# A macaron layer on one core: the passes reordered, attention dealt to them in whole blocks of 128 tokens

## The chip, the cores and the metric

The kernel runs on 1 core of a Trainium2 chip. The metric is the device time of one execution in microseconds, the median of several runs. Everything is float32; products are made of float32 values split in a high and a low half.

## What is computed

The reference, cut to what matters (B 4, S 1024, D 512, 16 heads of 32, hidden size 2048):

```
def attn(x):                      # per token: 16 heads attend to each other
    q, k, v = (x @ wq.T), (x @ wk.T), (x @ wv.T)      # each (b, s, 16, 32)
    q, k = apply_rope(q), apply_rope(k)
    scores = einsum('bshd,bstd->bsht', q, k) / sqrt(32)
    return einsum('bsht,bstd->bshd', softmax(scores), v).reshape(b, s, 512) @ wo.T

def ffn(x):                       # fwht: normalized Walsh-Hadamard transform
    hidden = fwht(silu(x @ W1.T) * (x @ W3.T))
    return hidden @ W2.T

x = x + 0.5 * ffn(layernorm(x))
x = x + attn(layernorm(x))
x = x + 0.5 * ffn(layernorm(x))
```

The scores of a token are 16 x 16, over its own heads. So attention has no matrix product to speak of beside its projections, and its scores and mixtures are made on VectorE.

## The kernel before

**Tiles, blocks, passes.** The 4096 tokens are 8 tiles of 512; a tile has 4 blocks of 128 tokens. Each tile goes through a feed-forward twice, so there are 16 passes over the feed-forward weights, numbered 0 to 15. Pass 0 also prepares the weights (the transform is folded in the down weights, all are split in two halves and stored to memory). The order is tile 0's first feed-forward, then by turns the first one of tile i (pass 2i-1) and the second one of tile i-1 (pass 2i), and at last the second one of tile 7 (pass 15).

**A pass.** It has 16 steps, one for each 128 of the 2048 hidden values. TensorE does the up step (24 matmuls of 128x512 into PSUM `gu`: W1 and W3, 4 parts of the depth, 3 products of halves), and then the down step of the step before (12 matmuls into `acc`). Between them ScalarE makes silu (L573, `gated`), VectorE the product with the linear half (L807), ScalarE the high half (L579, `hid`) and VectorE the low half (L811). The down step waits for the low half. The up step n waits for the product of step n-2, whose PSUM it takes. The weights come from memory in each step over the queue of SP.

**Between two passes** ("the gap") stand, for the tiles that are due, the transposes of the normalised rows (L386), the output projection of a tile's attention (`wo`), the projections of queries, keys and values (`qkv`), and on VectorE the sums, the norms (L831, L836, L840; GpSimd makes the inverse root, L737 and L739), the low halves (L817) and the rotation of queries and keys (`rope`, L1005 to L1010).

**Attention of a block** is 16 pieces on VectorE: 8 of scores (a product of 128x1024, L257, and a sum over 32, L862), then the softmax (L870, L871, the exponential on ScalarE L614, L877, L878), then 8 of mixtures (L260 and L864), and a division (L882). The pieces stand between the feed-forward's instructions. `ffn` of the loop's passes has two blocks (`attention_sub`, 8 steps each). Passes 1 and 14 have all four blocks of a tile (`attention_dense`): there GpSimd makes 12 of each block's 16 products (`SHARED`, `shared_products`) and VectorE sums them.

**What sets the order.** Each engine's program is written out by hand and waits on counting semaphores; passes 2 to 13 stand in a loop over tiles (`Fori(2, LAST)`), whose body is `iteration`.

Of the kernel before, what the change touches and what calls it, by code (L numbers as in the profile page):

```python
# [7 lines left out]
FP32 = mybir.dt.float32  # L8
# [6 lines left out]
HEADS = 16  # L15
# [17 lines left out]

class Count:


    def __init__(self, sem):
        self.sem, self.start, self.k = sem, 0, 0

    def mark(self, ins):  # L40
        ins.then_inc(self.sem, 1)
        self.k += 1
        return self.start + self.k
# [9 lines left out]
def build(nc, x, up_raw, w2t, attn_raw, inv_freq, hadamard, identity, out):  # L53
    ctx = ExitStack()
    with ctx:
# [14 lines left out]

        down_stage = w_attn[:].rearrange("p m a k n -> p (m a k n)").rearrange("p (a n) -> p a n", a=HT)

        xt = [sb(f"xt{i}", [P, 2, KT, TOK], FP32R) for i in range(2)]
        hid = sb("hid", [P, 2, 2, TOK], FP32R)
        gated = sb("gated", [P, 2, TOK])
        x_in = sb("x_in", [P, SUBS, D])
        x_mid = sb("x_mid", [P, SUBS, D])
        x_out = sb("x_out", [P, SUBS, D])
# [10 lines left out]
        stats = sb("stats", [P, SUBS, 6])  # L89
        mean_var = sb("mean_var", [P, SUBS, 2])  # L90
        rstd = sb("rstd", [P, SUBS])
        eps = sb("eps", [P, SUBS])
        mixed = sb("mixed", [P, HEADS, HD])
        carrier = sb("carrier", [P, 64])
        minus_half = sb("minus_half", [P, SUBS])
# [6 lines left out]
        s_hada = sem("s_hada")  # L102
        s_w2 = [sem(f"s_w2_{c}") for c in range(len(W2_CUTS))]
        s_x = sem("s_x")
        s_first_x = [sem(f"s_first_x{s}") for s in range(SUBS)]
        s_attn_raw = [sem(f"s_attn_raw{m}") for m in range(4)]
# [5 lines left out]
        s_freq_out = sem("s_freq_out")  # L112

        s_tabs = sem("s_tabs")
# [23 lines left out]
        s_var_0 = sem("s_var_0")  # L138
        s_eps_0 = sem("s_eps_0")
        s_rstd_0 = sem("s_rstd_0")  # L140
        s_ln = sem("s_ln")
        s_ln_sub = sem("s_ln_sub")
        s_xt_ps = sem("s_xt_ps")
        s_xt_hi = sem("s_xt_hi")
        s_xt_lo = sem("s_xt_lo")
# [3 lines left out]
        s_mid = sem("s_mid")  # L149
# [7 lines left out]
        s_shared = sem("s_shared")  # L157
        s_summed = sem("s_summed")
# [6 lines left out]

        LAST = TILES - 1
# [4 lines left out]
        HADAMARD_FROM = 7  # L173

        def raw_hidden(n):

            at = RAW.index(n)
            if at < SUBS:
                return x_out[:, at, :]
            if at < 2 * SUBS:  # L180
                return x_mid[:, at - SUBS, :]
            return prod[:, 2, (at - 2 * SUBS) * TOK:(at - 2 * SUBS + 1) * TOK]
# [17 lines left out]
        def turns_at_once(l):  # L200

            return l + 1 if isinstance(l, int) and l == 0 else l

# [3 lines left out]

        EVEN = ((3, 3, 2), (1, 3, 2, 2, 0))  # L210
        PIECES = HEADS // 2
# [6 lines left out]
        def dense_order():  # L218

            order = []  # L220
            for s in range(SUBS):
                order += [(s, u) for u in range(AHEAD if s else 0, PIECES)]
                if s + 1 < SUBS:
                    order += [(s + 1, u) for u in range(AHEAD)]
                order += [(s, PIECES + u) for u in range(PIECES)]

            at = order.index((SUBS - 1, PIECES))
            held = order.index((SUBS - 1, AHEAD)) - AHEAD
            return order[:held] + order[held + AHEAD:at] + order[held:held + AHEAD] + order[at:]

# [3 lines left out]
        def tok_at(slot):  # L234

            if isinstance(slot, int):
                return heads(tok[:, slot, :])
            return tok[:, bass.ds(slot, 1), :].rearrange("p o (h d) -> p (o h) d", h=HEADS)

        def values_at(slot):  # L240

            if isinstance(slot, int):
                return tok[:, slot, :].rearrange("p (d t) -> p d t", d=HD)
            return tok[:, bass.ds(slot, 1), :].rearrange("p o (d t) -> p (o d) t", d=HD)

        def product_buffer(b):

            if b < 3:
                return prod[:, b, :]
            return tok[:, 12 + 2 * (b - 3):14 + 2 * (b - 3), :].rearrange("p a n -> p (a n)")  # L250

        def unit_products(eng, s, u, buf, half=0):

            g = 2 * (u % PIECES)
            if u < PIECES:
                q, k = tok_at(2 * s), tok_at(2 * s + 1)
                return eng.tensor_tensor(product_buffer(buf).rearrange("p (h t d) -> p h t d", h=2, t=HEADS),  # L257
                                         wide(q[:, g:g + 2, None, :], 2, HEADS), wide(k[:, None, :, :], 1, 2), ALU.mult)
            v = values_at(8 + s)
            return eng.tensor_tensor(product_buffer(buf).rearrange("p (h d t) -> p h d t", h=2, d=HD),  # L260
                                     wide(scores[:, half, g:g + 2, None, :], 2, HD), wide(v[:, None, :, :], 1, 2), ALU.mult)
# [6 lines left out]
        def _(sp):  # L268
# [9 lines left out]
            for s in range(SUBS):  # L278
                sp.dma_start(x_in[:, s, :], x_v[0][:, s, :]).then_inc(s_first_x[s], 16)
# [6 lines left out]
            sp.dma_start(freq[:], wide(inv_freq.rearrange("(a f) -> a f", a=1), 0, P)).then_inc(s_freq_out, 16)  # L286
# [9 lines left out]
            for j in range(HT):  # L296
                keep_up(j, j % 2, j + 2 < HT)

# [45 lines left out]
            with sp.Fori(1, 2 * TILES) as b:  # L344
                weights(b)
# [3 lines left out]
        def _(pe):  # L349
# [6 lines left out]
            def xt_ready(build, k, needed=True):  # L356

                if needed:
                    pe.wait_ge(s_xt_lo, 4 * build + k + 1)

            def up(n, u, X, build=None):
                for w in range(2):
                    for k in range(KT):
                        xt_ready(build, k, build is not None and w == 0)
# [17 lines left out]
            def transposes(src, bank, ks):  # L382

                for k in ks:
                    for s in range(SUBS):
                        ins = nc.tensor.transpose(bank[:, k, s * P:(s + 1) * P], tok[:, src(s), k * P:(k + 1) * P], ident[:])  # L386
                    ins.then_inc(s_xt_ps, 1)

            def transposes_by_sub(src, bank, sub_ready):

                for s in range(SUBS):
                    sub_ready(s)
                    for k in range(KT):
                        ins = nc.tensor.transpose(bank[:, k, s * P:(s + 1) * P], src(s, k), ident[:])
                        if s == SUBS - 1:
                            ins.then_inc(s_xt_ps, 1)

            def sub_normed(l):

                return lambda s: pe.wait_ge(s_ln, l + 1) if s == SUBS - 1 else pe.wait_ge(s_ln_sub, (SUBS - 1) * l + s + 1)  # L400

            def normed(s, k):
                return tok[:, 12 + s, k * P:(k + 1) * P]

            def ffn(b, X, x_build, before_build=None, src=None, dense=None, values=None):

                n0 = HT * b

                def up_step(jj, u, x_build=None):
                    pe.wait_ge(s_up_loaded[u], 16 * (HT // 2 * (b - 1) + jj + 1))
                    up(n0 + 2 * jj + u, u, X, x_build)

                def down_step(jj, u, first, last):
                    pe.wait_ge(s_down_loaded[u], 16 * (HT // 2 * (b - 1) + jj + 1))
                    down(n0 + 2 * jj + u, u, first, last)

                if values is not None:
                    pe.wait_ge(s_v, values - 2)  # L420
                up_step(0, 0, x_build)
                if values is not None:
                    pe.wait_ge(s_v, values)
                up_step(0, 1)
                pe.wait_ge(s_added, SUBS * b)
                down_step(0, 0, True, False)
                with pe.Fori(1, HT // 2) as jj:
                    for u in range(2):
                        pe.wait_ge(s_h, n0 + 2 * jj + u - 1)
                        up_step(jj, u)  # L430
                        down_step(jj - 1 + u, 1 - u, False, False)
                if dense is not None:
                    down_step(HT // 2 - 1, 1, False, True)
                    pe.wait_ge(s_h, n0 + HT)
# [813 lines left out]
```

## Time and profile before

| | |
|---|---|
| median of 3 runs | 2620.24 us (2619.89 to 2620.66) |
| profiled execution, own time | 2618.36 us |
| its span, first to last instruction | 2616.6 us |
| mean granted TensorE clock | 0.99 |
| TensorE matmuls busy | 97% of the span |
| VectorE busy | 76% |
| ScalarE busy | 21% |
| GpSimd busy | 12% |

Matmuls are pipelined, so that a busy share of TensorE says only that it was not idle. The distance from one matmul's start to the next says how long one takes.

### The profile page before, as it was taken

What the parts mean: (1) busy time and instruction counts of PE and PEld (TensorE: products, weight loads), DVE (VectorE), ACT (ScalarE), POOL (GpSimd) and SP (SyncE); (2) the same over time, 40 slices, a digit from 0 to 9 for tenths busy, and PEclk for the clock granted to TensorE, in tenths of its full rate; (3) what the DMA queues carried; (4) which work ended last, traced back from release to release, by engine and by line L of the source; (5) the groups of instructions that cost most, each with busy time, mean ns of one, the idle gap of its engine ahead of it and who ended that gap; (6) DMA issues with size and microseconds to landing.
All of it is one profiled execution on the core that took longest, in us unless ns stands there. A gap on an engine that the chain in (4) does not pass through costs nothing.

```text
span 2616.6 us, 32355 instructions
## 1 busy us (share of the span) xinstructions
PE 2544.9 (97%) x11328; PEld 2099.1 (80%) x11328; DVE 1991.0 (76%) x2494; ACT 539.6 (21%) x829; POOL 320.9 (12%) x164
## 2 busy tenths in 40 slices
PE   8989989999999999999999999999999999998799
PEld 6867768888888888888888888888888888877687
DVE  7668997777887777778777778877778777879712
ACT  3312221122111211222112211112121121122111
POOL 0046850000000000000000000000000000168400
PEclk9999999999999999999999999999999999999899
DMA  9643423555335551455515554255533555144254
GB/s 307 233 177 123 167 96 113 192 205 193 115 142 194 198 195 74 181 193 199 192 64 193 204 192 168 88 193 208 192 136 120 192 209 192 73 150 155 97 192 168
DMA packets 91644, 437.05 MB, mean 167 GB/s; under 512 B 8896, under 2 KB 15296, under 8 KB 58304
## 3 DMA queue, kind: packets, MB, share of 16 engines
q1 hardware_dynamic: 83616, 420.65, 43.9%
q10 hardware_dynamic: 7968, 15.73, 1.7%
q8 instruction: 21, 0.34, 0.1%
q14 instruction: 39, 0.32, 0.0%
HBM read 402.79 MB, written 33.55 MB: 167 GB/s over the span
## 4 chain that ended last, share of the span: by engine, by line
PE 83%; DVE 14%; issue 1%; SPq 1%; POOL 1%; DMA 0%; ACT 0%; POOLq 0%; DVEq 0%; ACTq 0%
PE gu L352 19%; PE gu L354 19%; PE gu L353 19%; PE acc L352 8%; PE acc L354 8%; PE acc L353 8%; DVE mixed L864 3%; DVE prod L260 2%; DVE scores L862 2%; DVE hid L811 1%; PE gu L386 1%; DVE prod L257 1%; DVE gated L807 1%; DVE xt L817 1%; PE acc L463 1%
## 5 line engine op out<-in xcount | busy, mean ns | idle before, releaser
L352 PE MATMUL gu<-xt,w_up 128*128 128x512 f32 x2048 | 800.6, 391 | 3.6 <-DVE xt L817 3.6
L353 PE MATMUL gu<-xt,w_up 128*128 128x512 f32 x2048 | 798.2, 390 | 0.0
L354 PE MATMUL gu<-xt,w_up 128*128 128x512 f32 x2048 | 797.9, 390 | 0.0
L352 PEld LDWEIGHTS gu<-xt,w_up 128*128 128x128 f32 x2048 | 385.4, 188 | 85.8 <-DVE xt L817 3.0
L807 DVE TENSOR_TENSOR gated<-gated,gu 128x512 f32<-128x512 f32 x240 | 164.0, 683 | 375.6 <-ACT gated L573 375.6
L354 PEld LDWEIGHTS gu<-xt,w_up 128*128 128x128 f32 x2048 | 385.2, 188 | 80.3
L353 PEld LDWEIGHTS gu<-xt,w_up 128*128 128x128 f32 x2048 | 385.4, 188 | 80.0
L352 PE MATMUL acc<-w_down,hid 128*128 128x512 f32 x960 | 383.7, 400 | 35.6 <-DVE hid L811 35.6
L573 ACT ACTIVATE gated<-gu 128x512 f32<-128x512 f32 x240 | 143.5, 598 | 1149.5 <-PE gu L354 1149.4
L353 PE MATMUL acc<-w_down,hid 128*128 128x512 f32 x960 | 380.0, 396 | 0.0
L354 PE MATMUL acc<-w_down,hid 128*128 128x512 f32 x960 | 379.9, 396 | 0.0
L260 DVE TENSOR_TENSOR prod<-scores,tok 128x1024 f32<-128x1024 f32 x216 | 295.3, 1367 | 0.8
L864 DVE TENSOR_REDUCE mixed<-prod 128x64 f32<-128x1024 f32 x224 | 265.6, 1212 | 1.7
L862 DVE TENSOR_REDUCE scores<-prod 128x32 f32<-128x1024 f32 x224 | 264.7, 1210 | 0.5
L257 DVE TENSOR_TENSOR prod<-tok 128x1024 f32 (+1 forms) x200 | 252.4, 1262 | 6.9 <-DVE scores L862 0.8
L352 PEld LDWEIGHTS acc<-w_down,hid 128*128 128x128 f32 x960 | 183.8, 191 | 81.2 <-DVE hid L811 35.2
L737 POOL TENSOR_TENSOR rstd<-mean_var,eps 128x4 f32<-128x4 f32 x23 | 4.6, 199 | 1925.2 <-DVE mean_var L836 1925.2
L579 ACT ACTIVATE hid<-gated 128x512 fp32r<-128x512 f32 x240 | 152.0, 633 | 423.9 <-DVE gated L807 421.8
L354 PEld LDWEIGHTS acc<-w_down,hid 128*128 128x128 f32 x960 | 184.1, 192 | 39.2
L353 PEld LDWEIGHTS acc<-w_down,hid 128*128 128x128 f32 x960 | 184.2, 192 | 37.6
L811 DVE TENSOR_TENSOR hid<-gated,hid 128x512 fp32r<-128x512 f32 x240 | 177.2, 738 | 44.7 <-ACT hid L579 44.7
L352 PE MATMUL gu<-w_attn,xt 128*128 128x512 f32 x512 | 201.3, 393 | 8.0 <-DVE xt L817 3.8
(122 smaller groups left out, 2188.3 us busy)
## 6 DMA issues: line engine op xcount, KB each, us to landing
w_up<-up_pairs SPq DMA_DIRECT2D x240, 1024.0 KB, 4.8
w_down<-down_pairs SPq DMA_DIRECT2D x240, 512.0 KB, 3.4
up_pairs<-w_up SPq DMA_DIRECT2D x16, 1024.0 KB, 4.8
prod<-up_raw SPq DMA_DIRECT2D x16, 512.0 KB, 5.8
down_pairs<-w_attn SPq DMA_DIRECT2D x4, 2048.0 KB, 17.7
x_in<-x ACTq DMA_DIRECT2D x7, 1024.0 KB, 5.3
out<-x_out ACTq DMA_DIRECT2D x7, 1024.0 KB, 4.6
tok<-attn_raw SPq DMA_DIRECT2D x4, 1024.0 KB, 18.8
```

What stands on the lines that cost most here:

```text
L257: return eng.tensor_tensor(product_buffer(buf).rearrange("p (h t d) -> p h t d", h=2, t=HEADS), wide(q[:, g:g + 2, None, :], 2, HEADS), wi ...
L260: return eng.tensor_tensor(product_buffer(buf).rearrange("p (h d t) -> p h d t", h=2, d=HD), wide(scores[:, half, g:g + 2, None, :], 2, HD ...
L352: nc.tensor.matmul(o, w_hi, m_hi, start=first, stop=False)
L353: nc.tensor.matmul(o, w_hi, m_lo, start=False, stop=False)
L354: return nc.tensor.matmul(o, w_lo, m_hi, start=False, stop=last)
L386: ins = nc.tensor.transpose(bank[:, k, s * P:(s + 1) * P], tok[:, src(s), k * P:(k + 1) * P], ident[:])
L573: nc.scalar.activation(gated[:, u, :], gu[:, 2 * u, :], ACT.Silu).then_inc(s_silu, 1)
L579: nc.scalar.activation(hidden(u)[0], gated[:, u, :], ACT.Copy).then_inc(s_hid_hi, 1)
L807: nc.vector.tensor_tensor(gated[:, u, :], gated[:, u, :], gu[:, 2 * u + 1, :], ALU.mult).then_inc(s_h, 1)
L811: nc.vector.tensor_tensor(low, gated[:, u, :], high.bitcast(FP32), ALU.subtract)\
L862: return nc.vector.tensor_reduce(scores[:, half, g:g + 2, :], product_buffer(buf).rearrange("p (h t d) -> p h t d", h=2, t=HEADS), AX.X, A ...
L864: return nc.vector.tensor_reduce(mixed[:, g:g + 2, :], product_buffer(buf).rearrange("p (h d t) -> p h d t", h=2, d=HD), AX.X, ALU.add)
```

## The change

**The passes** follow a table `PASSES` (1 or 2 for the feed-forward, and the tile): 1.0, 1.1, 1.2, 2.0, 1.3, 2.1, 1.4, 2.2, 1.5, 2.3, 1.6, 1.7, 2.4, 2.5, 2.6, 2.7. So pass 2 is now a first feed-forward and pass 3 the second one of tile 0. `WO_AT` says in which gap a tile's output projection stands. Where the pass behind that gap is the second feed-forward of the same tile (`LATE`, passes 3, 5, 7, 14, 15), its norm is made in the gap (`late_gap`); for all other passes the norm of the next tile is made beside the steps of the pass before, in steps 8, 9, 11 and 12 (`beside`), and its transposes stand before the last down step (`early_gap`).

**Attention** is dealt by `LAST_SUB` (the last block whose projections are made before pass p) and `UNITS_TO` (pieces done by the end of pass p). Each of the passes 1 to 14 has 32 pieces, two whole blocks, but passes 2, 5, 8 and 12, which have 48, three blocks. `AHEAD` is 0: no block is begun before the one ahead of it is done. All pieces are made on VectorE; the code for GpSimd's products is gone. A planner (`units_by_step`) spreads a pass's pieces over its steps 0 to 14. A block that is projected first in its gap has its norm made in the pass before where its tile allows it (`early_subs`, one or two blocks, steps 10 and 13).

**The rest.** Four tiles of residuals stay on the chip (`xs`) in place of `x_in`, `x_mid` and `x_out`, so ScalarE's copy of a tile (L660) is gone and a tile is loaded some passes ahead. All programs but the inner steps of TensorE and SP are written out with constant waits, without a loop. At the start TensorE runs 24 matmuls on zeros (`WARM`), and the second tile is loaded in the middle of pass 0.

```diff
+PASSES = ((1, 0), (1, 1), (1, 2), (2, 0), (1, 3), (2, 1), (1, 4), (2, 2),
+          (1, 5), (2, 3), (1, 6), (1, 7), (2, 4), (2, 5), (2, 6), (2, 7))
+WO_AT = {3: 0, 5: 1, 7: 2, 8: 3, 10: 4, 12: 5, 14: 6, 15: 7}
+LATE = tuple(p for p, t in WO_AT.items() if PASSES[p] == (2, t))
+LAST_SUB = (None, 2, 4, 6, 8, 11, 13, 15, 18, 20, 22, 24, 27, 29, 31)
+UNITS_TO = (0, 32, 80, 112, 144, 192, 224, 256, 304, 336, 368, 400, 448, 480, 512)
+AHEAD = 0
+def units_by_step(p):
+    mine, steps = list(UNITS.get(p, ())), []
+    beside = [0.0] * HT
+    if p + 1 < NP and p + 1 not in LATE:
+        for n, cost in ((X_STATS, 1.4), (X_STATS + 1, 2.0), (X_APPLY, 1.1), (X_APPLY + 1, 1.1)):
+            beside[n] += cost
+    beside[Q_STATS] += 0.85 * len(early_subs(p + 1))
+    beside[Q_APPLY] += 0.55 * len(early_subs(p + 1))
+    unit = 2.5
+    total, spent = sum(beside) + unit * len(mine), 0.0
+    for n in range(HT):
+        spent += beside[n]
+        now = []
+        while mine and n < STEPS and (n == STEPS - 1 or spent + unit / 2 <= total * (n + 1) / STEPS):
+            now.append(mine.pop(0))
+            spent += unit
+        steps.append(tuple(now))
...
-        SHARED = 3 * ((0, 1, 3, 4, 5, 6, 7, 9, 10, 12, 14, 15),) + ((0, 1, 3, 4, 5, 6, 7, 9, 10, 12, 13, 15),)
-        POOL_BUFFERS = 3
-        AHEAD = 4
...
+            pe.wait_ge(s_zeros, 1)
+            for _ in range(WARM):
+                nc.tensor.matmul(acc[:, 0, :], hid[:, 0, 0, 0:P], hid[:, 0, 0, :], start=True, stop=True)
...
+            def attention(p):
+                mine = UNITS.get(p, ())
+                free, made = [chain.k] * 2, {}
...
+                for at, (g, u) in enumerate(mine):
+                    if u == PIECES:
+                        row_sums(g)
+                    if at not in made:
+                        make(at)
+                    if at + 1 < len(mine) and mine[at + 1][1] not in (0, PIECES):
+                        make(at + 1)
+                    dve.wait_ge(s_dve, made.pop(at))
+                    free[at % 2] = chain.mark(unit_sum(g, u, at % 2))
+                    if u == PIECES - 1:
+                        shift(g, free[at % 2])
+                    if u == 2 * PIECES - 1:
+                        divide(g, free[at % 2])
+                    yield
...
+                for n in range(HT):
+                    u, count = n % 2, len(STEP_UNITS[p][n])
+                    dve.wait_ge(s_silu, n0 + n + 1)
+                    nc.vector.tensor_tensor(gated[:, u, :], gated[:, u, :], gu[:, 2 * u + 1, :], ALU.mult).then_inc(s_h, 1)
+                    unit(min(count, 1))
...
+                    dve.wait_ge(s_hid_hi, n0 + n + 1)
+                    high, low = hidden(u)
+                    nc.vector.tensor_tensor(low, gated[:, u, :], high.bitcast(FP32), ALU.subtract).then_inc(s_hid_lo, 1)
+                    unit(count - min(count, 1))
+                    beside(n)
```

`make` is a product into one of two buffers, `unit_sum` its sum. VectorE in pass 1, one step and the start of the next. Before, in a packed pass, with products that GpSimd has made (a sum that reads `tok` or `prod` without a product ahead of it):

```order
L807 TENSOR_TENSOR gated<-gated,gu 128x512
L862 TENSOR_REDUCE scores<-tok 128x32
L811 TENSOR_TENSOR hid<-gated,hid 128x512
L862 TENSOR_REDUCE scores<-tok 128x32
L257 TENSOR_TENSOR prod<-tok 128x1024
L862 TENSOR_REDUCE scores<-prod 128x32 x2
L807 TENSOR_TENSOR gated<-gated,gu 128x512
```

The change, same pass:

```order
L1381 TENSOR_TENSOR gated<-gated,gu 128x512
L1136 TENSOR_TENSOR prod<-tok 128x1024 x2
L1148 TENSOR_REDUCE scores<-prod 128x32
L1388 TENSOR_TENSOR hid<-gated,hid 128x512
L1136 TENSOR_TENSOR prod<-tok 128x1024
L1148 TENSOR_REDUCE scores<-prod 128x32
L1381 TENSOR_TENSOR gated<-gated,gu 128x512
```

Four sums and one product a step became two sums and their own products.

VectorE in pass 2 of the change, a step with four pieces of a block, between two products of the hidden values (L1381):

```order
L1381 TENSOR_TENSOR gated<-gated,gu 128x512
L1136 TENSOR_TENSOR prod<-tok 128x1024
L1148 TENSOR_REDUCE scores<-prod 128x32
L1388 TENSOR_TENSOR hid<-gated,hid 128x512
L1136 TENSOR_TENSOR prod<-tok 128x1024
L1148 TENSOR_REDUCE scores<-prod 128x32
L1136 TENSOR_TENSOR prod<-tok 128x1024
L1148 TENSOR_REDUCE scores<-prod 128x32
L1136 TENSOR_TENSOR prod<-tok 128x1024
L1148 TENSOR_REDUCE scores<-prod 128x32
L1381 TENSOR_TENSOR gated<-gated,gu 128x512
```

Before, the fullest steps of pass 2 have three pieces; now steps of three and four take turns through the whole pass, one piece between the product and the low half (L1388) and the others behind it.

## Rows read from the trace of the kernel before

**Rows 1.** The page: busy time, and the granted clock in 40 slices.

```profile
PE 2544.9 (97%) x11328; PEld 2099.1 (80%) x11328; DVE 1991.0 (76%) x2494; ACT 539.6 (21%) x829; POOL 320.9 (12%) x164
...
PEclk9999999999999999999999999999999999999899
```

**Rows 2.** Timeline of TensorE, down, up, down; last from the chain, a tile's transposes.

```profile
540.92 0.39 PE L352 MATMUL acc<-w_down,hid 128*128 128x512 f32 x1
...
543.64 0.39 PE L352 MATMUL gu<-xt,w_up 128*128 128x512 f32 x1
...
549.08 0.39 PE L352 MATMUL acc<-w_down,hid 128*128 128x512 f32 x1
...
712.73 1.75 PE acc L386 x16
```

**Rows 3.** Windows: passes 1, 14, one loop turn, a plain pass; clock, DMA last.

```profile
213.87:372.73 158.86, 141.66 (x576) 113.32 (x577) 153.05 (x135) 31.88 (x46) 131.60 (x48) 0.94 0.44 159
2298.34:2458.00 159.66, 141.52 (x578) 113.54 (x577) 152.29 (x133) 32.00 (x45) 124.64 (x45) 0.94 0.44 158
400.60:712.73 312.13, 312.03 (x1410) 259.13 (x1409) 243.12 (x312) 63.84 (x97) 3.62 (x6) 1.00 0.46 168
...
552.00:684.00 132.00, 132.00 (x592) 109.58 (x591) 102.69 (x114) 27.76 (x42) 0.00 (x0) 1.00 0.54 198
```

**Rows 4.** Waits, whole run, TensorE: total, times, longest.

```profile
PE acc L352 <- DVE hid L811: 35.6, 15, 5.1
```

**Rows 5.** Timeline of TensorE behind passes 1 and 14, the idle time in brackets.

```profile
376.32 0.50 PE L352 MATMUL gu<-w_attn,xt 128*128 128x512 f32 x1 [1.68 <-DVE xt L817]
...
2461.59 0.50 PE L352 MATMUL gu<-w_attn,xt 128*128 128x512 f32 x1 [1.68 <-DVE xt L817]
```

**Rows 6.** Timeline of VectorE in a plain pass: a step, then a softmax.

```profile
570.87 0.68 DVE L807 TENSOR_TENSOR gated<-gated,gu 128x512 f32<-128x512 f32 x1
571.47 1.22 DVE L257 TENSOR_TENSOR prod<-tok 128x1024 f32 x1
...
579.09 0.68 DVE L807 TENSOR_TENSOR gated<-gated,gu 128x512 f32<-128x512 f32 x1
...
584.93 0.42 DVE L870 TENSOR_REDUCE head_max<-scores 128x16 f32<-128x256 f32 x1
...
585.72 0.68 DVE L807 TENSOR_TENSOR gated<-gated,gu 128x512 f32<-128x512 f32 x1
...
588.83 0.42 DVE L877 TENSOR_REDUCE head_sum<-scores 128x16 f32<-128x256 f32 x1 [1.03 <-ACT scores L614]
...
589.51 1.23 DVE L260 TENSOR_TENSOR prod<-scores,tok 128x1024 f32<-128x1024 f32 x1
```

**Rows 7.** Groups by line and form, whole run: busy us, mean ns, idle before.

```profile
L257 DVE TENSOR_TENSOR prod<-tok 128x1024 f32 x192 | 234.1, 1219 | 6.9 <-DVE scores L862 0.8
...
L573 ACT ACTIVATE gated<-gu 128x512 f32<-128x512 f32 x240 | 143.5, 598 | 1149.5 <-PE gu L354 1149.4
...
L257 DVE TENSOR_TENSOR prod<-tok 128x1024 f32<-128x1024 f32 x8 | 18.3, 2292 | 0.0
...
L882 DVE TENSOR_TENSOR tok<-mixed,head_sum 128x512 f32 x24 | 16.6, 692 | 0.8
```

**Rows 8.** Timeline of VectorE in a gap: a tile's statistics and its normalisation.

```profile
417.07 2.46 DVE L831 BATCH_NORM_STATS2 stats<-x_in 128x6 f32<-128x512 f32 x4
...
421.47 1.92 DVE L840 TENSOR_SCALAR tok<-x_in,mean_var,rstd 128x512 f32<-128x512 f32 x4 [1.40 <-POOL rstd L739]
```

**Rows 9.** Timeline of TensorE in the last gap.

```profile
2477.49 3.65 PE L394 MATMUL acc<-ident,tok 128*128 128x128 f32 x16 [4.68 <-DVE tok L840]
```

**Rows 10.** Pass 0: TensorE's first and third up steps; a low half, from the chain.

```profile
15.71 0.80 PE L352 MATMUL gu<-xt,w_up 128*128 128x512 f32 x1 [2.56 <-DVE xt L817]
...
29.15 0.40 PE L352 MATMUL gu<-xt,w_up 128*128 128x512 f32 x1
...
27.66 1.22 DVE w_up L1015
```

More of the change, by code:

```diff
@@ new lines @@
+UNITS = units_by_pass()
+X_STATS, X_APPLY, Q_STATS, Q_APPLY = 8, 11, 10, 13
+STEPS = HT - 1
+def units_by_step(p):
[15 more added lines that the diff above has]
+        steps.append(tuple(now))
+    assert not mine
+    return tuple(steps)
@@ new lines, with exps @@
+STEP_UNITS = {p: units_by_step(p) for p in range(1, NP)}
+def exps():
+    place = {}
+    for p in range(1, NP):
+        for n, units in enumerate(STEP_UNITS[p]):
+            for g, u in units:
+                place[g, u] = p, n
+    behind, ahead = {}, {}
+    for g in range(TILES * SUBS):
+        made, used = place[g, PIECES - 1], place[g, PIECES]
+        if made == used:
+            behind.setdefault(made, []).append(g)
+        else:
+            ahead.setdefault((made[0], made[1] + 1), []).append(g)
+    return behind, ahead
@@ new lines, with transposed @@
+EXP_BEHIND, EXP_AHEAD = exps()
+X_ORDER = (2, 3, 0, 1)
+def transposed():
+    order = [("x", 0, k) for k in range(KT)]
+    order += [("q", g, 0) for g in new_subs(1)] + [("x", 1, k) for k in range(KT)]
+    for p in range(2, NP):
+        new = new_subs(p)
+        att = [("a", WO_AT[p], k) for k in range(KT)] if p in WO_AT else []
+        if p in LATE:
+            order += att + [("q", g, 0) for g in new[:2]] + [("x", p, k) for k in range(KT)]
+        else:
+            order += [("q", g, 0) for g in early_subs(p)] + [("x", p, k) for k in X_ORDER]
+            order += [("q", g, 0) for j, g in enumerate(new[:2]) if not is_early(p, j)] + att
+        order += [("q", g, 0) for g in new[2:]]
+    return {key: at for at, key in enumerate(order)}
@@ new lines, with normed_groups, group_subs @@
+TP = transposed()
+def normed_groups():
+    order = [("x", 0)] + [("q", g) for g in new_subs(1)] + [("x", 1)]
+    for p in range(2, NP):
+        if p not in LATE:
+            order.append(("x", p))
+        if early_subs(p):
+            order.append(("e", p))
+        late = [("x", p)] if p in LATE else []
+        order += late + [("q", g) for j, g in enumerate(new_subs(p)) if not is_early(p, j)]
+    return order
+def group_subs(key):
+    if key[0] == "x":
+        return tuple(range(SUBS))
+    return early_subs(key[1]) if key[0] == "e" else (key[1],)
@@ new lines, with ln_of_sub, sub_slots @@
+GROUPS = normed_groups()
+GROUP = {key: at for at, key in enumerate(GROUPS)}
+LN_FROM = dict(zip(GROUPS, itertools.accumulate([len(group_subs(key)) for key in GROUPS], initial=0)))
+def ln_of_sub(g):
+    p = next(p for p in range(1, len(LAST_SUB)) if g in new_subs(p))
+    j = new_subs(p).index(g)
+    return LN_FROM["e", p] + early_subs(p).index(g) + 1 if is_early(p, j) else LN_FROM["q", g] + 1
+def sub_slots():
+    free, held, slots = {a: None for a in range(12)}, {}, {}
+    for p in range(1, len(LAST_SUB)):
+        for g in list(held):
+            if len(held[g]) == 3 and all((g, 2 * PIECES - 1) != unit for q in range(p, len(LAST_SUB)) for unit in UNITS[q]):
+                for a in held[g][1:]:
+                    free[a] = ("s", g)
+                held[g] = held[g][:1]
+        if p in WO_AT:
+            for g in range(SUBS * WO_AT[p], SUBS * WO_AT[p] + SUBS):
+                free[held.pop(g)[0]] = ("a", WO_AT[p])
+        for g in new_subs(p):
+            mine = [a for a in free][:3]
+            slots[g] = tuple((a, free.pop(a)) for a in mine)
+            held[g] = tuple(mine)
+    return slots
@@ new lines, in x_of, with ln_column, ln_columns, normed @@
+        def x_of(g):
+            return residual(g // SUBS)[:, g % SUBS, :]
+        def ln_column(key):
+            if key[0] == "x":
+                return 0
+            if key[0] == "q" and key[1] in new_subs(1):
+                return 4 + key[1]
+            return 4 if key[0] == "e" else 6
+        def ln_columns(key):
+            return set(range(ln_column(key), ln_column(key) + len(group_subs(key))))
+        def normed(s):
+            return tok[:, 12 + s, :]
+        def sub_normed(g):
+            p = next(p for p in range(1, len(LAST_SUB)) if g in new_subs(p))
+            j = new_subs(p).index(g)
+            if p == 1:
+                return normed(j)
+            return prod[:, 2, (j % 2) * D:(j % 2 + 1) * D]
@@ L398, in sub_normed @@
[L398 to L434, printed above, removed]
-                    transposes_by_sub(lambda s, k: tok[:, 2 * s, k * P:(k + 1) * P], gu,
-                                      lambda s: pe.wait_ge(s_attn, dense + s + 1))
-                    return
-                if before_build is not None:
-                    before_build()
-                    pe.wait_ge(s_h, n0 + HT - 1)
-                    transposes(src, gu, (0, 1))
-                    pe.wait_ge(s_h, n0 + HT)
-                    transposes(src, gu, (2, 3))
-                down_step(HT // 2 - 1, 1, False, True)
@@ new lines, in sub_high, with values @@
+            def sub_high(g):
+                split_high(sub_split(g)[0], sub_bank(g).rearrange("p (k t) -> p k t", k=KT), "q", g, 0)
+            def values(g):
+                slot, before = SLOTS[g][2]
+                if before is not None and before[0] == "a":
+                    act.wait_ge(s_tp, TP["a", before[1], KT - 1] + 1)
+                if before is not None and before[0] == "s":
+                    act.wait_ge(s_attn, before[1] + 1)
+                act.wait_ge(s_v_ps, g + 1)
+                nc.scalar.activation(tok[:, slot, :], v_bank(g), ACT.Copy).then_inc(s_v, 1)
@@ new lines, in gap @@
+            def gap(p):
+                new = new_subs(p)
+                if p in LATE:
+                    attention_high(p)
+                    for g in new[:2]:
+                        sub_high(g)
+                    for k in range(KT):
+                        x_high(p, k)
+                else:
+                    for k in X_ORDER:
+                        x_high(p, k)
+                    for j, g in enumerate(new[:2]):
+                        if not is_early(p, j):
+                            sub_high(g)
+                    if p in WO_AT:
+                        attention_high(p)
+                for j, g in enumerate(new):
+                    values(g)
+                    if j == 0 and len(new) > 2:
+                        sub_high(new[2])
@@ new lines, in sub_low, with ln_stats, ln_means @@
+            def sub_low(g):
+                high, low = sub_split(g)
+                split_low(low, sub_bank(g).rearrange("p (k t) -> p k t", k=KT), high, "q", g, 0)
+            def ln_stats(key, s, src):
+                at = ln_column(key) + s
+                return chain.mark(nc.vector.bn_stats(stats[:, at, :], src))
+            def ln_means(key, mark, same_columns):
+                dve.wait_ge(s_dve, mark)
+                if same_columns is not None:
+                    dve.wait_ge(s_ln, LN_FROM[same_columns] + len(group_subs(same_columns)))
+                for s in range(len(group_subs(key))):
+                    at = ln_column(key) + s
+                    ins = nc.vector.bn_aggr(mean_var[:, at, :], stats[:, at, :])
+                ins.then_inc(s_var, 1)
@@ L1212, in hadamard_128, with j_of @@
+            def j_of(p, g):
+                return new_subs(p).index(g)
+            feed_forward(1)
+            for p in range(2, NP):
+                if p in LATE:
+                    late_gap(p)
+                else:
+                    early_gap(p)
+                feed_forward(p)
+            for s in range(SUBS):
+                add_sum(NP - 1, s)
 def hadamard_128():
```

1121 lines of the change are left out of this document (589 added, 532 removed).

## The prediction

> **What bounds the kernel now.** I read the page first: TensorE is busy 97% of the span, VectorE 76%, GpSimd 12%, and the granted clock is 9 or more in every slice but one [rows 1]. So almost all of the time is matmuls, and what a change can move is the rest. Next the timeline of TensorE in a plain pass: the first matmul of a down step starts at 540.92, the first of the following up step at 543.64, the next down step at 549.08 [rows 2]. Twelve matmuls take 2.72 us, 36 take 8.16, so one is 0.2267 us and a pass of 16 steps 130.6. Then the stretches. The 16 transposes of a tile take 1.75 us [rows 2]. One turn of the loop (two passes, 1344 matmuls and 64 transposes) is 312.13 us with TensorE busy for 312.03 of it, at clock 1.00 [rows 3]: the plain passes have nothing to lose. Passes 1 and 14 are different. They hold four blocks of attention each, take 158.86 and 159.66 us for the work of 130.6, at a mean clock of 0.94, and VectorE is busy for 153.05 and 152.29 of it [rows 3]. VectorE is the bound there, and the list of waits says so: TensorE waits for the low half of the hidden values 15 times, 35.6 us, up to 5.1 each [rows 4]. After each of these passes TensorE waits another 1.68 us [rows 5]. That is all the attention costs today: 28.3 + 29.1 + 3.4 = 60.8 us.
>
> In a plain pass VectorE is busy for 102.69 us of 132 [rows 3]: two blocks leave some 29 us free. This is the number that the change turns on.
>
> **The change, part by part.**
>
> *Passes 1 and 14 hold two blocks.* They become plain passes, 130.6 us each. I take off the whole 60.8. This needs that a two-block pass without the old code is still hidden. Its VectorE work for steps 0 to 14: 32 pieces, each a product and a sum. A step from 570.87 to 579.09 holds the product and low half of the hidden values and three pieces [rows 6]; behind a product of 128x512 the next instruction starts 0.6 us later, so a piece is (8.22 - 1.2) / 3 = 2.34 us. 32 pieces are 75 us, 15 steps' own two instructions 18, the two softmaxes 6, norms 7: 106 against 15 x 8.16 = 122.4. Hidden on average. Within a step: from the end of an up step to the low half go silu 0.6 [rows 7], product 0.68, one piece 2.34 and a low half like the product, 4.3 us, while TensorE has 5.44 us of the next up step to do. 1.1 us are in hand. I cost it at nothing; the rival "short passes wait" prices it otherwise.
>
> *Passes 2, 5, 8 and 12 hold three blocks, on VectorE alone.* For pass 5, whose successor's rows and two early blocks are also normalised in it:
> - 48 pieces x 2.34 = 112.3 us;
> - per block the maximum and subtraction from 584.93 to 585.72, 0.79, the row sum and reciprocal from 588.83 to 589.51, 0.68 [rows 6], the division 0.69 [rows 7]: 3 x 2.16 = 6.5;
> - the wait for the exponential, 1.03 us in the plain pass [rows 6]. Two of three blocks have theirs issued in the same step, so 2; the third stands behind the next silu, which is early when VectorE is late;
> - the step's own two instructions, 15 x 1.2 = 18;
> - the next tile's statistics 2.46 and its normalisation 1.92 [rows 8], with 0.4 for the means 4.8; two early blocks, half of that, 2.4.
>
> The sum is 146.0 us for steps 0 to 14. To the start of the last down step comes silu before (0.7) and the last product, copy and low half behind (2.1): 148.8. TensorE alone needs for the same stretch 122.4 us and the transposes of a tile and two blocks, 1.75 + 2 x 0.44: 125.1 (rounded up). Excess 23.7 us. Pass 12 is alike. Pass 8 has one early block, 1.2 less work and 0.4 less transposes: 22.9. Pass 2 has no next tile to normalise (the one after it is late), 4.8 and 0.9 less: 19.8. Sum of the four: 90.1 us. Nothing is carried over into the gap between passes: the pieces of a pass end in its step 14, and VectorE's work in the gap (a block's rope is the like of six instructions of 0.6 us, 3.6) lies beside 36 matmuls, 8.2 us, of projections a block.
>
> What could make that smaller: if all 29.3 us that VectorE has free in a plain pass could be used, the third block's 16 x 2.34 + 2.16 + 1.0 = 40.6 would push TensorE by 11.3 us alone, 45 for the four. But a part of that free time lies at the pass's first up step and in its last, where no piece stands. What could make it larger: passes 1 and 14 ran at a mean clock of 0.94 [rows 3], which is some 12% of 159 us at 1.2 instead of 2.4 GHz, 9.6 us of matmul time each. If it all lay on the path in each long pass, 4 x 9.6 = 38 us on top. The long pass leaves TensorE idle as these do, but VectorE sets the pace, so only the last down steps count: I take 0.5 each, 2 us.
>
> *GpSimd makes no products.* In passes 1 and 14 VectorE's own products took 2.29 us, in the plain ones 1.22 [rows 7]. After the change nearly all should take 1.22. The Trainium skill (SBUF — State Buffer, "Who interferes with whom") says that a VectorE instruction with two SBUF inputs contends with a GpSimd instruction that reads SBUF, which would make the two means one cause. By another cause, a crowded pass as such, the 48 products of a long pass would cost 1.07 us more each, 51 us a pass, and the sum would be some 200 us higher; the plain passes, with GpSimd idle and 1.22, speak against it.
>
> *A figure against my step.* The Trainium skill (TensorE: Matmul & The Clock Gate, "Wait — 56ns, not 53.3ns?") has warm matmuls of 512 columns start 215.7 ns apart. By it a pass would be 124.2 us, not 130.6, and each long pass would exceed TensorE by 6.4 us more, 26 in all. The rows say 226.7 and I keep them.
>
> *The gaps.* Projections are the same number of matmuls in all, only spread otherwise. In a late gap the norm's chain must fit under one query and key projection of 5.44 us. From the last output projection: sum, statistics, means, GpSimd, normalisation: in the last gap of today this leaves TensorE 4.68 us idle before its transposes [rows 9], with nothing to cover it; in the new order 5.44 us cover it. Zero, but with under 1 us to spare. In pass 5's gap the third block's projection waits for a rope that stands behind the norm of that third block on VectorE. Counted in instructions of 0.6 us, the second block's rope ends some 32.6 us into the gap, while TensorE has 30.3 us of matmuls before that projection: 2.3 us. The last gap (pass 15) has no cover in either order: zero change. The gap after pass 0 has one block less: zero beside the moved matmuls, within 3 us either way.
>
> *The start.* 24 matmuls on zeros run ahead of the first transposes. Today the first up step starts at 15.71 and the third at 29.15, while the third slab's low half, which that one needs, is made from 27.66 to 28.88 [rows 10]. So an earlier or faster start is worth 0.3 us at most. The second tile's load in the middle of pass 0 and the 1 us of setup: zero, up to 3 us dearer.
>
> *The unrolled code.* VectorE's and ScalarE's loops are written out. Their waits do not show any loop cost today (0.1 us idle in 312), so there is none to win.
>
> **The sum.** The profiled execution took 2618.4 us: 2618.4 - 60.8 + 90.1 + 2 + 2.3 = 2652.0. The median of the runs is 1.9 us above it. The short passes and the start may win or lose a microsecond. I say 2652.
>
> **The rivals.** 0.2% (5.2 us) is about what a measurement of this kernel can tell from no change.
> - *Forecast: the long passes are bound by VectorE at about 20 to 24 us each.* 2652; 2630 to 2675 with the small costs either way. Chance 0.62.
> - *The third block goes into VectorE's idle time.* The place is the same four passes, the price 11.3 us each: 2618.4 - 60.8 + 45 + 4.3 + 1.9 = 2609, faster. For it speaks that 29.3 us are free; against it that the order puts all pieces in steps 0 to 14, and that a step of 3.2 pieces and its share of the norms comes to 9.7 us against 8.16. It decides as soon as a long pass costs under 12.8 us (51 in all), which needs pieces of 2.1 us or less. Chance 0.10.
> - *The two sides cancel.* A long pass costs 12.8 to 15.4 us, which takes pieces of 2.15 us. 2620. Chance 0.08.
> - *Short passes wait as well.* Ten passes; in two steps of each a softmax stands between pieces. If the 1.1 us in hand is used up and each of these is 1 us late: 20 us more, 2672. TensorE's plain passes with 0.1 us idle and the same softmaxes speak against it. Chance 0.10.
> - *The clock falls in the long passes and it counts.* Up to 38 us more, 2690. Against it: TensorE waits there for VectorE, and half speed is hidden by the wait. Chance 0.10.
>
> Slower is the first and the last two, 0.82; same 0.08; faster 0.10. The range runs from 2622 to 2686.
>
> **What the changed profile would show.** Passes 1 and 14 at 130.6 us and without a wait of TensorE for the low half; four stretches of 147 to 151 us, in passes 2, 5, 8 and 12, in which VectorE is busy over 95% and TensorE waits some 1.5 us in every step; clock below 1.00 in them alone. VectorE's products all at 1.22. GpSimd without its 131.60 and 124.64 us in passes 1 and 14 [rows 3]. Wrong would be: long passes under 140 us (pieces cheaper than 2.34, or work in the gap), or waits in short passes, or a clock below 0.97 over the whole.

## The result

The changed kernel takes 2639.66 us, the median of 4 runs (2639.04 to 2641.03). The kernel before took 2620.06 beside it. The ratio is 1.0076, with a 95% interval of 1.0058 to 1.0093: slower by 19.6 us. The forecast was 2652, slower, with a range of 2622 to 2686. The profiled execution took 2639.04 us against 2618.36 before, 20.7 more; its span is 2637.3.

The page of the changed kernel: busy times, the clock, and the groups that answer to [rows 7].

```profile
PE 2552.0 (97%) x11352; PEld 2095.9 (79%) x11352; DVE 2018.9 (77%) x2570; ACT 523.8 (20%) x821; POOL 62.7 (2%) x90
...
PEclk9999999999999999999999999999999999999999
...
L551 PE MATMUL acc<-w_down,hid 128*128 128x512 f32 x960 | 384.0, 400 | 52.0 <-DVE hid L1388 51.0
...
L1136 DVE TENSOR_TENSOR prod<-tok 128x1024 f32<-128x1024 f32 x256 | 309.5, 1220 | 1.5
```

The shares of busy time [rows 1] hardly tell the two kernels apart: TensorE 97% and 97%. The wait of TensorE for the low half of the hidden values tells more: 51.0 us here, 35.6 before [rows 4].

Windows of the changed kernel, each from the first matmul of a pass to the start of its last down step: passes 2, 5, 8 and 12, then 3 and 1. Behind the length stand the busy time and the number of instructions of TensorE, of its weight loads, of VectorE, ScalarE and GpSimd, then the granted clock, the DMA share and GB/s.

```profile
353.22:499.05 145.83, 134.26 (x582) 108.03 (x580) 137.93 (x150) 30.12 (x45) 0.90 (x2) 0.99 0.48 173
857.51:1008.35 150.84, 136.10 (x590) 108.57 (x588) 145.03 (x168) 31.43 (x47) 2.11 (x4) 0.99 0.47 165
1361.30:1510.83 149.53, 134.54 (x585) 108.34 (x584) 142.88 (x161) 30.06 (x45) 1.95 (x4) 0.99 0.52 183
2017.58:2168.41 150.83, 136.93 (x590) 109.93 (x588) 144.28 (x165) 30.82 (x46) 2.10 (x4) 0.98 0.47 167
531.84:662.55 130.71, 130.65 (x589) 108.28 (x588) 105.58 (x127) 28.06 (x44) 2.10 (x4) 1.00 0.52 189
201.53:331.85 130.32, 130.26 (x586) 107.84 (x584) 104.06 (x123) 27.71 (x43) 1.95 (x4) 1.00 0.52 190
```

The two kinds stand apart at once. In the last two windows, with two blocks, TensorE is busy for all but 0.06 us and VectorE for 80 or 81% of the stretch. In the first four, with three blocks, VectorE is busy for 95 or 96% (137.93 of 145.83, 145.03 of 150.84), TensorE idle for 12 to 15 us, and the stretch 15 to 20 us longer than with two. Pass 1 needs 130.32 us where the packed pass before took 158.86 [rows 3]; that window holds the last down step (2.72 us) and no transposes, this one 20 transposes (2.2 us) and no last down step, so the two are comparable within a microsecond.

How VectorE's time goes in a long pass is seen in its timeline, pass 5 of the changed kernel: its first product, a step of four pieces, the step behind it with a block's softmax, and the product of the last step.

```profile
863.78 0.69 DVE L1381 TENSOR_TENSOR gated<-gated,gu 128x512 f32<-128x512 f32 x1 [4.74 <-ACT gated L917]
...
873.04 0.68 DVE L1381 TENSOR_TENSOR gated<-gated,gu 128x512 f32<-128x512 f32 x1
...
883.54 0.68 DVE L1381 TENSOR_TENSOR gated<-gated,gu 128x512 f32<-128x512 f32 x1
...
885.84 0.42 DVE L1157 TENSOR_TENSOR scores<-scores,head_max 128x256 f32<-128x256 f32 x1
886.18 0.69 DVE L1388 TENSOR_TENSOR hid<-gated,hid 128x512 fp32r<-128x512 f32 x1
886.78 0.41 DVE L1164 TENSOR_REDUCE head_sum<-scores 128x16 f32<-128x256 f32 x1
...
1005.72 0.68 DVE L1381 TENSOR_TENSOR gated<-gated,gu 128x512 f32<-128x512 f32 x1
```

The step takes 10.50 us where TensorE needs 8.16 [rows 2]. Less the 1.2 of the step's own two instructions, four pieces are 9.30, 2.33 each. Such a step is rarer than "steps of three and four take turns" says: the planner gives pass 5 three steps of four pieces and twelve of three; pass 2 has four steps of four. Between the first and the last of these rows VectorE waits for nothing. The row sum (L1164) starts without idle time in front of it: the exponential is done while the low half (L1388) is made.

### The profile page after: what moved, and what is told of

Read it like the earlier page. It is cut to its first block, busy times and chain, and to the rows that moved or that the text cites. A ratio compares the mean times of both kernels' runs of the same rounds, so it can differ in the third digit from the quotient of the medians.

```text
span 2637.3 us, 30195 instructions
## 1 busy us (share of the span) xinstructions
PE 2552.0 (97%) x11352; PEld 2095.9 (79%) x11352; DVE 2018.9 (77%) x2570; ACT 523.8 (20%) x821; POOL 62.7 (2%) x90
## 4 chain that ended last, share of the span: by engine, by line
PE 76%; DVE 21%; issue 1%; SPq 1%; ACT 0%; DMA 0%; POOLq 0%; DVEq 0%; POOL 0%; ACTq 0%
PE gu L551 16%; PE gu L553 16%; PE gu L552 16%; PE acc L551 8%; PE acc L553 8%; PE acc L552 8%; DVE scores L1148 4%; DVE prod L1141 4%; DVE mixed L1150 4%; DVE prod L1136 4%; DVE hid L1388 1%; DVE gated L1381 1%; PE gu L584 1%; PE acc L584 1%; PE acc L639 1%
## 5 line engine op out<-in xcount | busy, mean ns | idle before, releaser
L1381 DVE TENSOR_TENSOR gated<-gated,gu 128x512 f32<-128x512 f32 x240 | 163.9, 683 | 370.2 <-ACT gated L917 369.5
L1136 DVE TENSOR_TENSOR prod<-tok 128x1024 f32<-128x1024 f32 x256 | 309.5, 1220 | 1.5
L1148 DVE TENSOR_REDUCE scores<-prod 128x32 f32<-128x1024 f32 x256 | 310.0, 1212 | 0.0
L1150 DVE TENSOR_REDUCE mixed<-prod 128x64 f32<-128x1024 f32 x256 | 309.8, 1212 | 0.0
L1141 DVE TENSOR_TENSOR prod<-scores,tok 128x1024 f32<-128x1024 f32 x256 | 307.7, 1212 | 1.2
L551 PEld LDWEIGHTS acc<-w_down,hid 128*128 128x128 f32 x960 | 181.7, 189 | 109.2 <-DVE hid L1388 54.9
L553 PEld LDWEIGHTS acc<-w_down,hid 128*128 128x128 f32 x960 | 182.1, 190 | 38.8
L552 PEld LDWEIGHTS acc<-w_down,hid 128*128 128x128 f32 x960 | 182.1, 190 | 35.5
L1388 DVE TENSOR_TENSOR hid<-gated,hid 128x512 fp32r<-128x512 f32 x240 | 163.9, 683 | 15.0 <-ACT hid L925 14.7
L551 PE MATMUL gu<-w_attn,sub_xt 128*128 128x512 f32 x232 | 92.2, 397 | 7.2 <-DVE sub_xt L1020 4.5
L552 PE MATMUL gu<-w_attn,sub_xt 128*128 128x512 f32 x232 | 91.0, 392 | 0.0
```

The source lines that it names most:

```text
L551: nc.tensor.matmul(o, w_hi, m_hi, start=first, stop=False)
L552: nc.tensor.matmul(o, w_hi, m_lo, start=False, stop=False)
L553: return nc.tensor.matmul(o, w_lo, m_hi, start=False, stop=last)
L1136: return nc.vector.tensor_tensor(prod[:, buf, :].rearrange("p (h t d) -> p h t d", h=2, t=HEADS), wide(q[:, h:h + 2, None, :], 2, HEADS), ...
L1141: return nc.vector.tensor_tensor(prod[:, buf, :].rearrange("p (h d t) -> p h d t", h=2, d=HD), wide(scores[:, g % 2, h:h + 2, None, :], 2, ...
L1148: return nc.vector.tensor_reduce(scores[:, g % 2, h:h + 2, :], prod[:, buf, :].rearrange("p (h t d) -> p h t d", h=2, t=HEADS), AX.X, ALU.add)
```

## The experiments

**1. The same work, dealt evenly.** The projections, norms and passes stay; only the pieces move, so that blocks are begun in one pass and ended in the next.

```diff
-UNITS_TO = (0, 32, 80, 112, 144, 192, 224, 256, 304, 336, 368, 400, 448, 480, 512)
+UNITS_TO = (0, 37, 73, 110, 144, 183, 219, 256, 293, 329, 366, 400, 438, 475, 512)
```

> The changed kernel with the same 512 pieces dealt evenly, 34 to 39 in each of the passes 1 to 14, blocks begun in one pass and ended in the next; projections, norms and passes stay where they are. Theory A (all of the loss is the four passes that VectorE bounds, 76.6 us in the profile): 2640 - 77, and up to 6 us given back where a pass has 38 or 39 pieces: 2563 to 2570. Rival B (the loss comes with the new order, its gaps and late norms, and VectorE's total work): no pass is relieved in sum, 2630 or more. Rival C (a block split over two passes costs waits of its own for the exponential and the values): 2580 to 2600.

Measured: 2566.74 us, ratio to before 0.9796 (0.9779 to 0.9812). Windows of the same passes 2, 5, 8 and 12, to the start of the last down step:

```profile
355.62:485.44 129.82, 129.76 (x581) 107.43 (x580) 110.47 (x125) 30.30 (x45) 0.90 (x2) 1.00 0.51 190
844.10:974.81 130.71, 130.65 (x589) 108.24 (x588) 122.40 (x145) 28.07 (x44) 2.10 (x4) 1.00 0.51 189
1327.65:1458.00 130.35, 130.28 (x585) 107.81 (x584) 115.81 (x134) 27.09 (x42) 1.95 (x4) 1.00 0.57 205
1966.02:2096.76 130.74, 130.68 (x589) 108.24 (x588) 119.56 (x140) 27.35 (x43) 2.10 (x4) 1.00 0.52 189
```

All four run at TensorE's pace, pass 5 with 39 pieces and VectorE busy for 94% of it. (The shortest, pass 2, has the fewest transposes.) TensorE's wait for the low half falls from 51.0 us to 2.7, here in the list of waits:

```profile
PE acc L551 <- DVE hid L1388: 2.7, 3, 1.5
```

Theory A holds. Rivals B and C fall: blocks split over two passes cost nothing that shows, and the new order costs no more than its gaps, whose waits are still there (4.5 us at a block's own norm, 3.4 at its rotation).

**2 and 3. Fewer pieces in the long passes.** 12, and then 6, of the 16 pieces of the third block are left out (blocks 4, 11, 18 and 27), so that its result is not complete. The others stay in their passes, and the planner spreads them anew over the steps. The edit of experiment 2; in experiment 3 the tuple is `(1, 2, 3, 9, 10, 11)`.

```diff
-        result[p] = mine
+        result[p] = [(g, u) for g, u in mine if not (g in (4, 11, 18, 27) and u in (1, 2, 3, 4, 5, 6, 9, 10, 11, 12, 13, 14))]
```

> The changed kernel with 12 of the 16 pieces of the third block left out in passes 2, 5, 8 and 12 (its scores and mixtures are not computed in full): 36 pieces in each of these passes. Theory A: VectorE is no longer the bound there, each of the four passes at its 132.4 to 133.3 us, 2640 - 77 = 2563, the same as with the pieces dealt evenly. If VectorE's total work counted by itself, it would be clearly faster than the even dealing, since it has 48 pieces (112 us of VectorE) less.

> The changed kernel with 6 of the 16 pieces of the third block left out in passes 2, 5, 8 and 12 (its scores and mixtures are not computed in full): 42 pieces each. Theory A with 2.33 us a piece: each long pass 14.0 us shorter, 20.4 becomes 6.4 and 16.3 becomes 2.3: 2640 - 56 = 2584. If the excess were the softmaxes, the waits for the exponential and the norms, and not the pieces, it would fall by less than half: 2605 or more.

Measured: 2563.41 us with 36 pieces (12 left out), 2584.18 with 42. The steps from 48 to 42 take 55.5 us off for 24 pieces, 2.31 us each, close to the 2.33 of VectorE's timeline. From 42 to 36 only another 20.8 are won, since the passes reach TensorE's pace on the way. With 48 pieces fewer in all, experiment 2 is only 3.3 us faster than the even dealing of all 512: pieces below the threshold are as good as free. Two windows with 42 pieces, passes 2 and 5:

```profile
353.04:485.10 132.06, 130.45 (x582) 107.29 (x580) 123.88 (x138) 30.15 (x45) 0.90 (x2) 1.00 0.51 187
842.16:979.36 137.20, 132.32 (x590) 107.90 (x588) 131.08 (x156) 31.43 (x47) 2.10 (x4) 1.00 0.52 184
```

They exceed the windows of the even dealing by 2.2 and 6.5 us.

**4. Without the matmuls on zeros.**

```diff
-        WARM = 24
+        WARM = 0
```

> The changed kernel without the 24 matmuls on zeros at the start. In its profile the first up step starts 2.4 us earlier than in the kernel before, but TensorE then waits 4.7 us for the third slab of weights and runs at half clock from 39.4 to 46.2 us. Theory: without them the third up step starts at 29.1 again and no half clock follows, 2 to 3 us faster, 2637. Rival (the half clock comes from the second tile's load or something else in pass 0): same or up to 1 us slower, 2640.

Measured: 2638.89 us (2636.58 to 2639.29) against 2639.66 (2639.04 to 2641.03): the ranges overlap, and the medians are 0.8 us apart where 2 to 3 were expected, so the times alone do not tell. The profiles do. Timeline of TensorE in the changed kernel: the first and the third up step of pass 0, and the first of pass 1; then a window behind the third step's start.

```profile
13.32 0.47 PE L551 MATMUL gu<-xt,w_up 128*128 128x512 f32 x1 [1.18 <-DVE xt L1020]
...
28.98 0.77 PE L551 MATMUL gu<-xt,w_up 128*128 128x512 f32 x1 [4.53 <-issue]
...
201.53 0.39 PE L551 MATMUL gu<-xt,w_up 128*128 128x512 f32 x1
...
28.70:35.30 6.60, 6.32 (x15) 5.01 (x16) 6.53 (x11) 1.69 (x2) 0.00 (x0) 0.51 0.73 250
```

The same rows without the matmuls on zeros:

```profile
14.12 0.76 PE L551 MATMUL gu<-xt,w_up 128*128 128x512 f32 x1 [0.86 <-DVE xt L1020]
...
28.77 0.47 PE L551 MATMUL gu<-xt,w_up 128*128 128x512 f32 x1 [1.25 <-issue]
...
199.14 0.39 PE L551 MATMUL gu<-xt,w_up 128*128 128x512 f32 x1
...
28.70:35.30 6.60, 6.53 (x28) 5.13 (x29) 6.53 (x10) 2.46 (x4) 0.00 (x0) 1.00 0.77 264
```

With them the first matmul of the first up step takes 0.47 us, the next start 0.23 apart, and the first two up steps end sooner; without them it takes 0.76, and the next start 0.43 apart up to 18.9 us. But the third starts at 28.98 in place of 28.77: it waits for its weights either way, whose low half is done at 28.88 and at 28.67. TensorE is idle for 4.53 us, and then the granted clock is 0.51 in this window (1.2 GHz) and 15 matmuls are done, where without them it is 1.00 (2.4 GHz) and 28 are done. The other traces agree: in the same window, experiments 1, 2, 3 and 7, which have the 24 matmuls, show 0.65, 0.54, 0.59 and 0.50; experiment 6 and the kernel before, without them, show 1.00. Pass 1 starts 2.4 us later. (The times of the half clock in the expectation, 39.4 to 46.2, were counted from another zero than the other times and are 11 us too late; on the scale of the rows they are 28.3 to 35.1.)

**5. The kernel before, VectorE alone.** GpSimd makes no products in passes 1 and 14.

```diff
-        SHARED = 3 * ((0, 1, 3, 4, 5, 6, 7, 9, 10, 12, 14, 15),) + ((0, 1, 3, 4, 5, 6, 7, 9, 10, 12, 13, 15),)
+        SHARED = 4 * ((),)
```

> The kernel before with no product on GpSimd: in passes 1 and 14 VectorE makes all 64 pieces of its four blocks itself. If the slow products of these passes (2.29 us against 1.22) come from GpSimd working at the same time, VectorE's products take 1.22 there too, and the passes are bound by 64 x 2.33 + 4 x 2.2 + 16 x 1.2 + 3 = 180 us each, against 159: 2620 + 42 = 2662. If they come from the crowded pass as such, products stay at 2.3 and the passes take some 240 us: 2780. If GpSimd's help was cancelled by its contention: 2620.

Measured: 2659.43 us, ratio 1.0158 (1.0142 to 1.0173). Windows of passes 1 and 14, and the group of VectorE's products in them:

```profile
212.78:391.92 179.14, 144.38 (x576) 113.46 (x576) 173.39 (x182) 32.22 (x46) 0.00 (x0) 0.93 0.40 141
2316.79:2496.40 179.61, 147.85 (x576) 115.74 (x575) 172.42 (x180) 32.22 (x45) 0.00 (x0) 0.92 0.40 140
```

```profile
L257 DVE TENSOR_TENSOR prod<-tok 128x1024 f32<-128x1024 f32 x64 | 76.8, 1220 | 0.6
```

The products take 1.22 us in a packed pass as well, so the 2.29 of [rows 7] came from GpSimd's work at the same time, as the expectation has it. The windows are cut as in [rows 3]. The rule of the Trainium skill (SBUF — State Buffer, "Who interferes with whom"), that a VectorE instruction with two SBUF inputs contends with a GpSimd instruction that reads SBUF, agrees with this. And the help was worth its contention: 20 us a pass. The whole of 64 pieces by 2.33 and the small terms gives 180, measured are 179.1 and 179.6.

**6 and 7. The best of both.** Experiment 6 has both edits, 7 only the first; they ran on the same chip.

```diff
-UNITS_TO = (0, 32, 80, 112, 144, 192, 224, 256, 304, 336, 368, 400, 448, 480, 512)
+UNITS_TO = (0, 37, 73, 110, 144, 183, 219, 256, 293, 329, 366, 400, 438, 475, 512)
...
-        WARM = 24
+        WARM = 0
```

> The changed kernel with the pieces dealt evenly (34 to 39 in a pass) and without the 24 matmuls at the start. Theory: the gain of the even dealing and the 2.4 us of the start add: 2566.7 - 2.4 = 2564. Rival (the start's gain is lost in pass 0's chain before it reaches the end): 2566.5.

> The even dealing with the 24 matmuls kept, on the same chip as the run without them, for the difference between the two: 2566.7 again.

Measured: 2565.15 us (2564.42 to 2565.99) and 2566.65 (2566.04 to 2569.66); ratios to before 0.9796 (0.9782 to 0.9809) and 0.9806 (0.9792 to 0.9819). The ranges do not overlap, though only just: 1.5 us, a little less than the 2.4 of the profiles of experiment 4. The even dealing without the 24 matmuls is the fastest kernel here that computes everything, 53.9 us faster than the kernel before beside it and 74.5 faster than the change.

## Why the prediction was right

Its mechanism was: the packed passes 1 and 14 give back 60.8 us, four passes with three blocks become bound by VectorE and take more than that. Experiments 1 to 3 show it. The sum, 2652.0, was built on the profiled execution of before, and the changed kernel's took 2639.04, 13 us less; the 1.9 us from there to the median, which the rival's 2609 has, was left out of the forecast. Term by term, from the two profiles:

| term | forecast | measured |
|---|---|---|
| passes 1 and 14 | -60.8 | -60.8 |
| passes 2, 5, 8, 12 | +90.1 | +76.2 |
| half clock in the long passes | +2 | none seen on the path |
| wait in the gap before pass 5 | +2.3 | +2.7 |
| half clock in that gap | 0 | +1.6 |
| gaps before passes 2, 9 and 11 | 0 | +4.5 |
| start, pass 0 and the gap behind it | 0 | -3.7 |
| last gap | 0 | -0.2 |
| sum | +33.6 | +20.3 |

The profiled executions differ by 20.7; the other 0.4 I can't name. It is not the short passes: each takes 0.2 or 0.3 us more than its matmuls and transposes by [rows 2], but so does each pass of the loop before (312.13 us for two, 311.6 by these rows).

**The long passes were mis-sized by 13.9 us, 3.5 each.** I had 148.8 us from the end of the first up step to the start of the last down step of pass 5. The window has 150.84, less the 5.44 of that up step 145.4. TensorE's own part, 125.1, was right: pass 3 has the same transposes and 130.71 - 5.44 = 125.3. So the excess is 20.3, in pass 12 the same, in pass 8 19.4, in pass 2 16.2. VectorE's timeline has 141.94 us from the first product of pass 5 to the product of its last step, where 146.0 were forecast. Two of these 4.1 us are "the wait for the exponential [...], so 2". The timeline of pass 5 has none: where VectorE is late, ScalarE has finished silu and the high half before, and the exponential fits under the low half or the product that stands in front of the row sum. I took the wait from a plain pass, where VectorE is early. The changed kernel has ten such waits, of up to 1.0 us, all in passes with two blocks, and none in the twelve blocks of the long ones. The rest is small, and most of it in the pieces: the steps' own two instructions take 17.9 us (18), the softmaxes and divisions 6.1 (6.5), the norms 7.0 (7.2), which leaves 111.0 for 48 pieces, 2.31 each and not 2.34 (112.3). Experiment 3 has the same 2.31. Against this the two ends of the stretch take 0.7 us more than costed (0.83 for 0.7 in front, 2.63 for 2.1 behind).

**The short passes hide two blocks**, as forecast: 0.06 us idle in the windows of passes 1 and 3, and no wait for the low half in any of the other eight. The rival that they wait falls.

**The rival "the third block goes into VectorE's idle time"** asked for 11.3 us a pass. Measured are 16 to 20. Experiment 3 gives the true threshold. A long pass reaches TensorE's pace with 20.3 / 2.31 = 8.8 pieces fewer, at about 39 of 48, and experiment 1 runs 39 in pass 5 without excess. Of the third block's 16 pieces 7 are hidden and 9 are not. The free time at a pass's ends, that I left out of the bound, is indeed not used. (TensorE waits 11 times for the low half in pass 5, 14.7 us in all, not in every step as I had said.)

**The rival "the clock falls and it counts"** falls for the long passes, and holds in small in a gap. The clock was at 0.98 or 0.99 in the long windows, and experiment 3's slope, the same as VectorE's own price, leaves no room for it. Windows of the changed kernel, the half clock in pass 5, and the third block's 36 matmuls in the gap before it:

```profile
994.30:997.70 3.40, 3.40 (x10) 2.66 (x9) 3.37 (x5) 0.00 (x0) 0.00 (x0) 0.50 0.00 0
847.74:857.51 9.77, 9.77 (x36) 7.95 (x37) 2.48 (x4) 0.00 (x0) 0.00 (x0) 0.84 0.00 1
```

In the pass VectorE, which sets the pace, goes on without a wait. In the gap TensorE is the bound: behind a wait of 2.71 us the granted clock is 0.84 over these matmuls, and they take 9.77 us in place of 8.16. I had costed the wait and nothing for the clock behind it, so the sign "clock below 1.00 in them alone" was wrong.

**Three gaps were wrong by 1.5 us each.** Before passes 2, 9 and 11 a block's norm is made in the gap itself, and its projection stands right behind its four transposes, with nothing to cover the split into halves. I had costed these gaps at zero and had not followed them. In the gap before pass 5 the wait that I had worked out at 2.3 is there, at 2.71. Timeline of TensorE in the gaps before passes 2 and 5, and the last gap, which answers to [rows 9] (before, 4.68 us and another 0.86 behind the transposes):

```profile
342.21 0.47 PE L551 MATMUL gu<-w_attn,sub_xt 128*128 128x512 f32 x1 [1.50 <-DVE sub_xt L1020]
...
847.74 0.79 PE L551 MATMUL gu<-w_attn,sub_xt 128*128 128x512 f32 x1 [2.71 <-DVE tok L1119]
...
2499.17 3.68 PE L584 MATMUL acc<-ident,tok 128*128 128x128 f32 x16 [5.31 <-DVE tok L1052]
```

**The start went two ways.** Pass 1 begins at 201.53, before at 213.87 (the first window of [rows 3]): 12.3 us earlier, of which 36 matmuls and four transposes, 8.6, only moved to other gaps. That leaves 3.7, although the matmuls on zeros lose 2.4 (experiment 4). So pass 0 and the gap behind it are some 6 us better than I said. Most of it the traces name. Here are the window of 180 matmuls at the end of pass 0 and TensorE's longest waits behind it, in the kernel before:

```profile
121.03:168.59 47.56, 43.62 (x181) 34.44 (x179) 25.48 (x38) 8.25 (x15) 21.37 (x10) 0.96 0.72 283
...
PE gu L352 <- DVE carrier L797: 2.7, 1, 2.7
PE acc L487 <- DVE tok L1122: 1.7, 1, 1.7
PE gu L386 <- ACT tok L679: 0.8, 1, 0.8
```

And in the changed kernel:

```profile
123.18:169.20 46.02, 42.12 (x182) 33.31 (x180) 25.42 (x37) 8.26 (x15) 21.37 (x10) 1.00 0.75 292
...
PE acc L598 <- DVE tok L1052: 0.8, 1, 0.8
PE gu L551 <- DVE tok L1119: 0.6, 1, 0.6
```

The window is 1.5 us shorter, at a clock of 1.00 where it was 0.96, and the waits are 4 us less. Which part of the change took them away was not tried.

## What to carry to other kernels

When an engine is free for a fifth of every stretch, that time is spent stretch by stretch: work over the limit of one is not paid by the room in the next. Count the work in the smallest piece that can move, find how many pieces a stretch hides (39 here), and deal to that number, not to whole blocks; the same 512 pieces cost 73 us more in another dealing. And take a wait from a stretch of the same kind: one read where the waiting engine is early says nothing of one where it is late.

## What the runs showed of the hardware

With matmuls ahead of the real work the real ones started 0.23 us apart from the first step on, but here this cost time. They then ran out of weights, TensorE was idle for 4.53 us, and the granted clock was 0.51 for the next 6.6 us, where the work had no slack; without them the idle time was 1.25 us and the clock stayed at 1.00.

A wait on the path can cost more than itself: in the gap before pass 5 TensorE waited 2.71 us, and the 36 matmuls behind it took 1.6 us more than at the full clock.

A VectorE product of 128x1024 took 2.29 us beside GpSimd's products and 1.22 without them, in the same packed pass; the shared work was still 20 us a pass faster.
